# Waits of TensorE by halves and the place of VectorE's LayerNorm sums in a feed-forward, scan, feed-forward kernel

## What is computed

```python
x = x + 0.5 * ffn(layernorm(x))
x = x + mamba(layernorm(x))
x = x + 0.5 * ffn(layernorm(x))      # the same weights as the first
```

## Time and profile before

| | |
|---|---|
| median of three runs | 2841.28 us |
| the profiled execution, its own time | 2846.45 us |
| its span, first to last instruction | 2844.7 us |
| TensorE products busy | 2612.2 us, 92% |
| GpSimd busy | 2349.2 us, 83% |
| VectorE busy | 2218.2 us, 78% |
| ScalarE busy | 1499.8 us, 53% |
| DMA engines | 131 GB/s on average |
| mean granted clock of TensorE | 0.98 |

### The profile page before, as it was taken

The page is one execution under the profiler, slowest core; times in us unless marked ns, Lnnn a source line. Parts: engine busy times, 40 slices in busy tenths (PEclk is TensorE's granted clock), DMA queues, the critical chain, the costliest instruction groups (busy, mean ns, idle before and its releaser), DMA issues.

```text
span 2844.7 us, 39804 instructions
## 1 busy us (share of the span) xinstructions
PE 2612.2 (92%) x13597; PEld 1183.5 (42%) x13664; DVE 2218.2 (78%) x2933; ACT 1499.8 (53%) x3363; POOL 2349.2 (83%) x703
## 2 busy tenths in 40 slices
PE   4989999999999999898999989999999998888999
PEld 1444444444344444343444434444444433444444
DVE  8447878878888788787878878788788887887843
ACT  5355656565555554555555545555455454555521
POOL 2038988999999998899999989999899998988920
PEclk8999999999999999999999999999999999999999
DMA  5144444544454444544453445544454444453321
GB/s 217 55 113 131 138 126 130 158 147 129 135 143 133 145 122 140 133 135 139 135 162 114 136 134 155 152 125 126 140 157 143 135 127 125 137 138 126 99 63 52
DMA packets 303520, 373.50 MB, mean 131 GB/s; under 512 B 148435, under 2 KB 220243, under 8 KB 303318
## 3 DMA queue, kind: packets, MB, share of 16 engines
q1 hardware_dynamic: 286422, 337.40, 40.2%
q10 hardware_dynamic: 16896, 33.56, 4.0%
HBM read 234.05 MB, written 103.29 MB: 119 GB/s over the span
## 4 chain that ended last, share of the span: by engine, by line
PE 35%; DVE 33%; ACT 8%; DMA 8%; DVEq 7%; issue 5%; POOL 2%; ACTq 1%; SPq 1%; POOLq 0%
DVE mreg L1136 18%; PE pv L544 12%; PE po L544 7%; PE pv L548 6%; PE po L548 4%; ACT pA L922 3%; DMA delta_scratch<-mreg 3%; DMA mreg<-xnT_scratch 2%; PE py L710 2%; DVE pv L1097 2%; DVEq L1052 2%; PE pv L673 2%; DVE sel L1105 2%; DVE sel L1094 2%; DVEq L1102 2%
## 5 line engine op out<-in xcount | busy, mean ns | idle before, releaser
L512 POOL TENSOR_TENSOR mreg<-mreg 128x2048 f32<-128x2048 f32 x256 | 1161.6, 4538 | 70.8 <-ACT hst L908 70.6
L1136 DVE TENSOR_TENSOR_SCAN mreg<-pA,hst,mreg 128x512 f32<-128x512 f32 (+1 forms) x1024 | 1038.6, 1065 | 77.9 <-ACT hst L908 58.1
L922 ACT ACTIVATE pA<-mreg,nA 128x512 f32<-128x512 f32 (+1 forms) x1280 | 742.4, 596 | 458.6 <-DVE mreg L1136 415.9
L502 POOL TENSOR_TENSOR mreg<-mreg 128x1024 f32<-128x1024 f32 x340 | 795.8, 2365 | 223.4 <-DMA mreg<-delta_scratch 209.9
L544 PE MATMUL pv<-wA,xT 128*128 128x512 f16 x2016 | 471.9, 389 | 59.9 <-ACT xT L829 49.0
L544 PE MATMUL po<-wB,uT 128*128 128x512 f16 x2016 | 472.1, 383 | 15.6 <-DVE xin L1060 10.9
L544 PE MATMUL po<-wW,xT 128*128 128x512 f16 x2016 | 467.4, 380 | 6.5 <-issue 4.5
L496 POOL TENSOR_TENSOR mreg<-mreg 128x2048 f32<-128x2048 f32 x86 | 390.2, 4537 | 20.8 <-issue 20.8
L544 PEld LDWEIGHTS pv<-wA,xT 128*128 128x128 f16 x2016 | 196.0, 100 | 343.3 <-ACT xT L829 96.1
L1078 DVE TENSOR_REDUCE n<-sel 128x32 f32<-128x512 f32 x128 | 87.0, 680 | 306.5 <-ACT sel L837 306.4
L544 PEld LDWEIGHTS po<-wB,uT 128*128 128x128 f16 x2016 | 191.3, 98 | 293.5 <-issue 71.7
(11 more groups left out here) (132 smaller groups left out, 2376.4 us busy)
## 6 DMA issues: line engine op xcount, KB each, us to landing
mreg<-delta_scratch SPq DMA_DIRECT2D x256, 512.0 KB, 6.0
delta_scratch<-mreg ACTq DMA_DIRECT2D x128, 256.0 KB
xin<-x SPq DMA_DIRECT2D x32, 512.0 KB, 5.2
x_scratch<-xin SPq DMA_DIRECT2D x32, 512.0 KB, 3.9
xnT_scratch<-auxs SPq DMA_DIRECT2D x32, 512.0 KB, 2.9
mreg<-xnT_scratch SPq DMA_DIRECT2D x64, 256.0 KB, 7.0
yT_scratch<-mreg SPq DMA_DIRECT2D x64, 256.0 KB, 2.3
uT<-yT_scratch SPq DMA_DIRECT2D x32, 512.0 KB, 4.6
```

The costliest lines, as they stand in the source:

```text
L502: pool.tensor_tensor(h[:, half * n:half * n + n, :], u, b.broadcast_to([P, n, c.width]), ALU.mult).then_inc(s_bm, 1)
L512: pool.tensor_tensor(h, h, by_c, ALU.mult).then_inc(s_cm, 1)
L922: last = nc.scalar.activation(dst[:, part, :], src[:, part, :], ACT.Exp, scale=nA[:, m:m + 1])
L1136: last = V.tensor_tensor_scan(h, split(pA[:, i % 2, :], c)[:, part, :], h, before, ALU.mult, ALU.add)
```

## The change

Three places in the lists. TensorE's `experts` waits for the first half of the high parts ahead of third 0 and for the second half ahead of third 1, where it waited for both ahead of third 0; the wait for both ahead of third 2 goes, that for the low parts stays. In TensorE's unit the second half of `y_blocks` moves behind the dense product's third (1, 1), and the two waits ahead of `routed` (for the copies of row `l` and for both halves of `add_y`) go. On VectorE, the LayerNorm sums of a kind 2 row move from behind scan 9 to behind scan 6, ahead of `delta(a, 0)` and of scans 7, 8 and 9; for a kind 1 row they stay.

```diff
--- before.py
+++ after.py
@@ -605,8 +605,9 @@
                                          start=False, stop=False)
 
             def experts(b, nb, third):
+                if nb == 0 and third < 2:
+                    pe.wait_ge(s_xhi, b.u * 2 + 1 + third)
                 if nb == 0 and third != 1:
-                    pe.wait_ge(s_xhi, b.u * 2 + 2)
                     pe.wait_ge(s_xlo, b.u * 2 + (1 if third == 0 else 2))
                 last = product(pv[:, nb, :], xT, wA, nb, third, True, True)
                 if third == 2:
@@ -729,17 +730,13 @@
                     if late:
                         pe.wait_ge(s_nc, late.w * 2 + 2)
                     y_blocks(y, 0)
+                base(a, 1, 1)
                 if y:
                     y_blocks(y, 1)
-                base(a, 1, 1)
                 base(a, 1, 2)
                 states(a, 1)
                 if late:
                     scan_products(a, late, y)
-                if late:
-                    pe.wait_ge(s_nc, late.w * 2 + 2)
-                if y:
-                    pe.wait_ge(s_ya, y.v * 2 + 2)
                 routed(a, 0, 0)
                 if late:
                     turn_products(late)
@@ -1172,9 +1169,11 @@
                 if b and b.kind == 2:
                     add_y(b, 1)
                 scans(5, 7)
+                if b and b.kind == 2:
+                    unit_stats(b)
                 delta(a, 0)
                 scans(7, 10)
-                if b:
+                if b and b.kind == 1:
                     unit_stats(b)
                 result(a, 0)
                 scans(10, 14)
```

## The result

| | before | after |
|---|---|---|
| median (4 runs each, side by side) | 2840.01 us | 2865.57 us |
| lowest and highest | 2836.82, 2844.68 | 2861.64, 2869.53 |
| the profiled execution, its own time | 2846.45 us | 2867.26 us |
| its span | 2844.7 us | 2865.5 us |
| mean granted clock of TensorE | 0.980 | 0.972 |

The changed kernel is slower: the ratio is 1.0088, with a 95% interval of 1.0076 to 1.0100. That is 25.6 us between the medians, where 16.5 was forecast. Between the two profiled executions it is 20.8 us, because the one of before lies 6.4 us above the median of the table and the one of after 1.7.

A forecast was written before the change was run, and what follows sets the result against it. In y units the ring of waits through VectorE's scans, not TensorE, was taken as the bound. Terms of 19.4 + 3.3 - 6.2 gave 16.5 us slower, from a median of 2841.3 to 2857.8 us, range 2826 to 2874.

The forecast's parts named there:

- four signs: Among those forecast: prepare directly behind decay 11, a 2.1 us stall before scan 12, waits for xn about 15 us longer.
- step 1: Sums ahead of scans 7 to 9 on VectorE: prepare, behind decay 11, comes later; 19.4 us slower in all.
- the fourteen units: Units 17, 19, 21, 25, 27, 32, 34, 38, 40, 42, 48 to 51: 0.68 us slower each, together 9.5.
- the six: Units 53, 54, 56 to 59, with two-row tiles: 0.86 us slower each, together 5.2.
- three double-tile units: Units 36, 44 and 52: delta stores and the second tile's load come 1.57 us later each, 4.7 together.
- Step 2: TensorE's wait by halves at experts: eight units keep 0.28 to 1.08 us each, 6.2 us faster in all.
- Step 3: Later y_blocks and dropped waits ahead of routed on TensorE: 3.3 us slower, all in units 60 to 62.
- The clock: TensorE's clock falls: gained and lost counted as equal, 0; bounds 9 us slower and 5 us faster.
- A: TensorE's stalls are the bound: faster, 2805 or 2811 us, smaller version 2826; chance 0.20 with that version.
- B: Gains and losses meet: step 2 keeps 15 us, step 1 costs 15; 2844 us, no change; chance 0.13.
- C: Delta step's shift spreads: GpSimd late in seven more units (11 us), 7 more clock falls (9); 2878 us; chance 0.12.
- D: Dropped waits do nothing, as others meet them: true for the copies' wait, otherwise part of B; no own chance.

The follow-up runs named there:

- sums-only run: Only the LayerNorm sums of kind 2 rows moved ahead of the delta step and scans 7 to 9, against the kernel before: 2867.65 us, ratio 1.0098.
- halves-only run: Only TensorE's experts waits half by half for the high parts, against the kernel before: 2838.51 us, ratio 0.9999.
- the run of that part alone: Only the second half of y_blocks moved behind third (1, 1) and the two waits ahead of routed gone, against the kernel before: 2839.87 us, ratio 1.0002.
- copies-first order: Against the kernel before, the two fp16 copies put ahead of decay 14, the magnitudes and the softplus for kind 2 rows: 2841.26 us, ratio 1.0003.

## Why the prediction was right, and where its sizes were off

**Direction and mechanism: right.** VectorE has no idle time ahead of scan 9, decay 11 waits for scan 9, and `prepare` waits for decay 11. Each of the four signs named for step 1 is in the rows: `prepare` without a wait, 2.08 us of stall before scan 12, 16.8 us more of waits for `xn` (forecast 15), `xn` 0.64 to 0.68 us later in nine of the fourteen units with single-row tiles. That decay 11 is the link was shown by putting `prepare` ahead of it, which took back 17.6 of the 29.3 us (20.0 by the groups' own medians of before).

**Step 1, by its terms.** The fourteen units were forecast at 9.5 and measured 9.7 in their first part, where the sums' delay stands; the six at 5.2 and 5.7. In the sums-only run these are 10.3 and 7.5. The three double-tile units were to pay 1.57 us each, 4.7 in all, as the stores of the first tile and behind them the load for the second come later. They came to 5.0, by that chain: from the second `squares` the stores start 1.7 us later in each, the load is issued 1.67, 1.65 and 2.15 us later, and it lands 0.3, 1.8 and 3.1 us later (units 36, 44 and 52). A single landing varies by about as much as the term: in the sums-only run they are 0.3, 0.9 and 1.9 us later, and the three units pay 1.7 us together; with the sums behind the delta step they are 1.4, 1.9 and 1.7 us later, and the units pay 3.2. That the sum came so near is partly luck. Units 15, 23 and 55, which I had at nothing, pay 1.1 together in after.

**Step 2: too large.** 6.2 us were forecast as a gain. In the halves-only run single units keep what was forecast or more (units 14, 22, 30, 37 and 54 as forecast, 38 0.40 in place of 0.69, and 31, 39 and 45, which I had at nothing, 0.68 each); the median shows at most 2.8. It is the term that was mis-sized most clearly. Some of it is lost again in units nearby, as the 1.64 us of unit 22's first part at half clock; where the rest goes isn't traced.

**Step 3: right in kind.** Waits for `uT` of about one us (forecast 0.6) come in 30 places and are covered by the wait for `xn`. In units 60 to 62, where there is no such cover, 2.5 us were measured and 3.3 forecast. In the run of that part alone the same units show 2.5 us, and the median does not tell it from none. The two removed waits are worth nothing, as said, since each was met by another.

**The clock: taken as 0, and not 0.** I had balanced falls lost against falls gained, with 9 us as the bound, and each fall at 1.3 us, where units 4, 27 and 25 show 1.68, 0.3 and 0. In the profiled pair the time at half clock rose by 42.1 us. At half speed that stretches up to 21 us of TensorE's work; how much of it lies on the path can't be read from one profile. Medians give a total of 25.6 where the steps without the clock give 16.5 (or 22.7 with step 2 at nothing). That leaves 3 to 9 us for the clock and for what else was not costed. The sums-only run, 29.3 us with 19.4 from step 1, leaves 10. The average over all executions puts 7 to 8 us on the clock for the change. No kernel here changed the clock alone over the whole run, so the share of the clock in these last us is an estimate and not shown.

**The rivals.** A (TensorE's stalls are the bound) is refuted three times: the halves, the removed waits and the copies-first order each took 10 to 25 us out of one row of TensorE's waits, and their ratios are 0.9999, 1.0001 and 1.0003. B's low price for step 1 is refuted by the sums-only run. C's 11 us for the delta step's spread do not show in its seven units (19, 27, 34, 42, 50, 51, 58): step 1 gave them 4.9 us, and whole they pay 3.4 in after and 6.4 in the sums-only run. C's clock falls did come. D is right for all of step 3 and for most of step 2.

**A slip without effect.** The longest wait for `xn` before is 9.8 us and stands at the very start of the kernel; the 9.6 us in unit 3 are a wait for another copy (`auxs`). No term used it.

## What to carry to other kernels

Before work is moved earlier on one engine, look at who takes it up and what stands ahead of that instruction in its own queue: sums that are ready five us too soon are worth nothing when their reader stands behind a decay that waits for the work they displaced. If the move is wanted, move the reader with it (17.6 to 20.0 of 29.3 us came back), and stop there: one step more and the other chain starved (29 and 51 us slower than before). A wait in the list of the busiest engine is not a price tag; here 25 us of such waits went with no gain, as the next one in the unit took their place. And before an experiment is read as having taken a term out, check in its trace that the term moved: with the sums behind the delta step the stores came as late as ever.

## What the runs showed of the hardware

That TensorE can run slower behind a stall was plain from unit 17 already; how little of it can reach the end was new to me. In unit 27 TensorE waited 2.40 us for `xn` before, and 2.83 after. Behind the wait of after the granted clock is 0.50 (the 1.2 GHz level), behind that of before it stayed at full. The same three groups of after:

```profile
1287.15 1.07 PE L536 MATMUL pv<-idf,xn 128*128 128x128 f32 x4 [2.83 <-ACT xn L821]
1288.01 1.06 PE L536 MATMUL pt<-idf,xn 128*128 128x128 f32 x4
1288.87 2.78 PE L548 MATMUL po<-wB,uT 128*128 128x512 f16 x8
```

Before they took 0.66, 0.60 and 1.89 us. The stretch from the first transpose to the `states` product behind them is 4.42 us long in place of 2.75, so 1.7 us were added; `experts` starts 1.3 us later by the same count, as it had waited 0.29 us for a low part before and waits for nothing now. At the next second `squares` 0.29 us are left. The other 1.0 is taken up in front of `squares`, which stands behind a decay in ScalarE's list: it starts 1.83 us behind the last product of `experts` before (at 1299.18) and 0.80 us behind it after (at 1303.90).

The longer wait is not what decides on the fall: in the run with the waits by halves the wait is 2.40 us, as before, and the clock falls all the same. There `xn` comes when it came before, and the unit takes 44.08 us in place of 43.77; in the change without the sums, with the same waits and no fall, it takes 43.77 too. So 0.3 us is what this fall costs in unit 27, where the same kind of fall costs 1.68 in unit 4.
